# Eight buffers for gathered rows in the one-expert stage, gathers issued five items ahead with indices read straight from the table

## The reference, cut to what matters

```
xn    = layernorm(x)                       # x: 16384 tokens x 512
D     = fractal_dimension(xn); filt = wave_filter(D, 512)
x1    = ifft(fft(xn) * filt).real          # a circular filter along the 512 features
lat   = x1 @ W_el + b_el                   # 24 bits a token
s     = x1 + golay_correct(lat > 0) @ W_le + b_le
top   = top_k(softmax(xn @ router_w.T), 2) # two of 8 experts a token
f     = sum over the two of (xn @ W[e] + prob[e]) * weight[e]
out   = x + s * silu(f)
```

## Time and profile before

| | us |
|---|---|
| median of 3 executions (lowest, highest) | 1233.81 (1232.29, 1234.79) |
| the profiled execution | 1223.38 |
| its span in the trace | 1221.6 |
| PE busy, DVE busy, POOL busy, ACT busy | 1127.6, 1098.6, 873.8, 510.6 |
| mean granted TensorE clock | 0.972 |

### The profile page before, as it was taken

How to read it: one execution, slowest core, us unless ns; L and a number is a source line. 1 busy time by engine, 2 the same in 40 slices (tenths; PEclk the granted TensorE clock), 3 DMA queues, 4 the chain that set the end, 5 groups by cost and what they waited for, 6 DMA issues and landing times. The chain is left out here.

```text
span 1221.6 us, 26833 instructions
## 1 busy us (share of the span) xinstructions
PE 1127.6 (92%) x6283; PEld 607.5 (50%) x6284; DVE 1098.6 (90%) x2664; ACT 510.6 (42%) x1151; POOL 873.8 (72%) x857
## 2 busy tenths in 40 slices
PE   5998988627979999999999999999999999999996
PEld 4565555313434455555555555555555555555553
DVE  7899999999876889899999998999999899999985
ACT  4476775555754333333333333333333333333332
POOL 1136556748884778788888877888888788888874
PEclk9999999858999999999999999999999999999998
DMA  8669999213545776666666666676666666667663
GB/s 327 242 210 215 209 198 171 52 47 107 168 145 155 166 167 176 167 176 172 171 175 176 172 171 173 171 177 169 177 172 171 169 179 172 174 169 178 176 166 107
DMA packets 216921, 208.74 MB, mean 171 GB/s; under 512 B 166271, under 2 KB 166271, under 8 KB 212786
## 3 DMA queue, kind: packets, MB, share of 16 engines
q1 hardware_dynamic: 184370, 124.31, 42.5%
q0 software_dynamic: 31360, 79.78, 22.2%
q10 hardware_dynamic: 1152, 4.19, 1.2%
HBM read 123.36 MB, written 47.11 MB: 140 GB/s over the span
## 5 line engine op out<-in xcount | busy, mean ns | idle before, releaser
L1429 PE MATMUL banks<-w_hi,arena 128*128 (+1 forms) x1136 | 432.7, 381 | 5.8 <-DMA arena<-arena 4.4
L1430 PE MATMUL banks<-w_lo,arena 128*128 (+1 forms) x1136 | 432.1, 380 | 0.0
L1431 PE MATMUL banks<-w_hi,arena 128*128 (+1 forms) x1136 | 431.9, 380 | 0.0
L711 ACT ACTIVATE arena<-xbuf,inf 128x512 f16<-128x512 f32 x156 | 112.6, 722 | 529.8 <-DVE xbuf L1219 525.4
L526 POOL DMA_INDIRECT inf<-token_info,gidx x156 | 204.4, 1311 | 54.0 <-issue 53.4
L524 POOL DMA_INDIRECT xbuf<-in_L_attn_x,gidx x156 | 186.7, 1197 | 78.4 <-issue 65.6
L564 POOL TENSOR_TENSOR xbuf<-xbuf 128x512 f32<-128x512 f32 x128 | 162.7, 1271 | 36.0 <-DVE xbuf L1288 28.6
L503 POOL DMA_INDIRECT pair_tokens<-tok,slot x112 | 109.4, 977 | 104.9 <-DVE slot L1052 72.9
L1429 PEld LDWEIGHTS banks<-w_hi,arena 128*128 128x128 f16 x1136 | 111.4, 98 | 134.3 <-issue 15.9
L1431 PEld LDWEIGHTS banks<-w_hi,arena 128*128 128x128 f16 x1136 | 111.6, 98 | 131.1 <-issue 1.9
L530 POOL DMA_INDIRECT out<-xbuf,sidx x128 | 142.4, 1113 | 40.7 <-issue 40.4
(11 more groups left out here) (304 smaller groups left out, 1737.7 us busy)
## 6 DMA issues: line engine op xcount, KB each, us to landing
xbuf<-in_L_attn_x SPq DMA_DIRECT2D x32, 1024.0 KB, 11.6
arena<-extra_sums SPq DMA_DIRECT2D x128, 256.0 KB, 2.7
arena<-in_L_ffn_expert_weights SPq DMA_DIRECT2D x8, 1024.0 KB, 10.9
extra_sums<-arena SPq DMA_DIRECT2D x28, 256.0 KB, 3.0
token_info<-info ACTq DMA_DIRECT2D x8, 512.0 KB
xbuf<-in_L_attn_x,gidx POOLq DMA_INDIRECT x156, 3.9
inf<-token_info,gidx POOLq DMA_INDIRECT x156, 2.9
arena<-arena SPq DMA_TRANSPOSE x128
```

What stands on the lines that cost most here:

```text
L711: nc.scalar.activation(hi4[ring(i, k)], uv2[:, b], ACT.Copy, scale=inf2[:, k, 1:2]).then_inc(hi_ready, 1)
L1429: mm(ps, hi[:, c], wh, start=(c == 0), stop=False)
L1430: mm(ps, hi[:, c], wl, start=False, stop=False)
L1431: end = mm(ps, lo[:, c], wh, start=False, stop=(c == C - 1))
```

## The change

The one-expert stage gets four more buffers for gathered rows: item n sits in seat `n % 8`. The far four seats lie in memory that only the main stage and the routing use (`x2_far` where the main stage keeps `o2` and `ysb2`, `inf_far` in `lat`). POOL issues five gathers before the first coefficient, and `extra_prepare(n)` gathers item n+5. The wait for `split_ready` and for the coefficient is now for item n-3 (the occupant eight items earlier), and for a main item for the one four items earlier. The indices are read from `tile_tok` itself, so ACT's copies into `gidx` go in this stage, 32 of them, and stay in the main stage. Amounts of work on DVE, PE and SP are unchanged.

```diff
+        x2_far = xb[:, 2 * U * E:3 * U * E].rearrange("p (s e) -> p s e", s=U)
...
+        inf_far = lat[:, 0:2 * NE, :].rearrange("p n t -> p (n t)").rearrange("p (s w) -> p s w", s=U)
...
+        def seat(i, k):
+            return (i * U + k) % (2 * U) if extra(i) else k
...
-            def gather(k):
-                tokens = bass.IndirectOffsetOnAxis(ap=gidx[:, k:k + 1], axis=0)
...
+            def fetch(i, k, tokens):
+                tokens = bass.IndirectOffsetOnAxis(ap=tokens, axis=0)
+                pool.indirect_dma_start(out=x_at(i, k), out_offset=None, in_=x_rows, in_offset=tokens,
+                                        bounds_check=N - 1, oob_is_err=False).then_inc(ld_x2[seat(i, k)], 16)
+                pool.indirect_dma_start(out=inf_at(i, k), out_offset=None, in_=info_dram, in_offset=tokens,
+                                        bounds_check=N - 1, oob_is_err=False).then_inc(ld_x2[seat(i, k)], 16)
+            def gather(n):
+                earlier = n - 2 * U if n < NX else n - U
+                after(pool, split_ready, earlier + 1)
+                after(pool, coef_ready, earlier + 1)
+                fetch(n // U, n % U, tile_tok[:, n:n + 1])
...
             def extra_prepare(n):
                 if n + 1 < NX:
                     extra_coef(n + 1)
-                pool.wait_ge(gidx_ready, n + U + 1)
-                pool.wait_ge(split_ready, n + 1)
-                pool.wait_ge(coef_ready, n + 1)
-                gather(n % U)
+                if n + AHEAD < NX + U:
+                    gather(n + AHEAD)
...
-            for k in range(U):
-                pool.wait_ge(gidx_ready, k + 1)
-                gather(k)
+            AHEAD = U + 1
+            pool.wait_ge(tiles_ready, 1)
+            for n in range(AHEAD):
+                gather(n)
             pool.wait_ge(live_ready, 1)
             extra_coef(0)
...
-                if n + 3 < NX:
-                    gather_index(*at(n // U + 1, k, 3))
-                elif n + 3 < NX + 2:
+                if NX <= n + 3 < NX + 2:
                     bits_part(*at(n // U, k, 3))
```

More of the change, by code:

```diff
@@ L314, in build @@
             "rows_ready rows_loaded rows_float exps_mm toks_mm diag_ready spread_mm tiles_ready")
-        ld_x2 = [sem(f"ld_x2_{i}") for i in range(U)]
+        ld_x2 = [sem(f"ld_x2_{i}") for i in range(2 * U)]
         ld_e = [sem(f"ld_e{i}") for i in range(U)]
@@ L378, in parts_free, with x_at, inf_at, x_loads @@
                 eng.wait_ge(turned[k % 2], turns_before(i, k))
+        def seat(i, k):
+            return (i * U + k) % (2 * U) if extra(i) else k
+        def x_at(i, k):
+            r = seat(i, k)
+            return x2[:, r] if r < U else x2_far[:, r - U]
+        def inf_at(i, k):
+            r = seat(i, k)
+            return inf2[:, r] if r < U else inf_far[:, r - U]
+        def x_loads(i, k):
+            if extra(i):
+                return 32 * ((i * U + k) // (2 * U) + 1)
+            return 32 * (i - XR + (NX + U) // (2 * U) + 1)
         def at(i, k, ahead):
@@ L536, in extra_coef @@
                 k = n % U
-                pool.wait_ge(ld_x2[k], 32 * (n // U + 1))
+                pool.wait_ge(ld_x2[seat(n // U, k)], x_loads(n // U, k))
                 after(pool, x_scaled, n - U + 1)
                 c = 8 + PATH[n][1]
-                G.tensor_tensor(cab[:, k, 0:1], inf2[:, k, c:c + 1], tq[:, 7, n:n + 1], ALU.mult).then_inc(coef_ready, 1)
+                G.tensor_tensor(cab[:, k, 0:1], inf_at(n // U, k)[:, c:c + 1], tq[:, 7, n:n + 1], ALU.mult).then_inc(coef_ready, 1)
             def main_coef(i, k):
                 m = (i - XR) * U + k
-                pool.wait_ge(ld_x2[k], 32 * (i + 1))
+                pool.wait_ge(ld_x2[k], x_loads(i, k))
                 if not (first_main(i) and k < 2):
@@ L568, in step @@
                 if not last:
-                    pool.wait_ge(gidx_ready, j + U + 1)
+                    pool.wait_ge(gidx_ready, j - NX + 1)
                 pool.wait_ge(o_ready, m + 1)
@@ L572, in step @@
                 if not last:
-                    gather(k)
+                    fetch(XR, k, gidx[:, k:k + 1])
                 scatter_out(k)
-            for k in range(U):
-                pool.wait_ge(gidx_ready, k + 1)
-                gather(k)
+            AHEAD = U + 1
+            pool.wait_ge(tiles_ready, 1)
+            for n in range(AHEAD):
+                gather(n)
             pool.wait_ge(live_ready, 1)
@@ L699, in bits_part @@
                 b = k % 2
-                act.wait_ge(ld_x2[k], 32 * (i + 1))
+                act.wait_ge(ld_x2[k], x_loads(i, k))
                 parts_free(act, i, k)
@@ L710, in high_part @@
                 parts_free(act, i, k)
-                nc.scalar.activation(hi4[ring(i, k)], uv2[:, b], ACT.Copy, scale=inf2[:, k, 1:2]).then_inc(hi_ready, 1)
+                nc.scalar.activation(hi4[ring(i, k)], uv2[:, b], ACT.Copy, scale=inf_at(i, k)[:, 1:2]).then_inc(hi_ready, 1)
             def turned_copy(n):
@@ L752, in step @@
                     gather_index(i + 1, k)
-            act.wait_ge(tiles_ready, 1)
-            for k in range(U):
-                gather_index(0, k)
             act.wait_ge(pad_ready, 1)
@@ L1210, in halves_of @@
                 n, b = i * U + k, k % 2
-                dve.wait_ge(ld_x2[k], 32 * (i + 1))
+                x, inf = x_at(i, k), inf_at(i, k)
+                dve.wait_ge(ld_x2[seat(i, k)], x_loads(i, k))
                 after(dve, hi_ready, n - 1)
@@ L1224, in low_part @@
                 parts_free(dve, i, k)
[L1225 removed]
+                V.scalar_tensor_tensor(lo4[ring(i, k)], uv2[:, b], inf_at(i, k)[:, 1:2], hi4[ring(i, k)], ALU.mult,
                                        ALU.subtract).then_inc(split_ready, 1)
```

12 lines of the change are left out of this document (3 added, 9 removed).

## The result

The changed kernel took 1237.26 us (median of 20 runs) against 1231.98 us for before (20 runs beside them): ratio 1.0041, interval 1.0025 to 1.0057. The forecast was no change; it is slower by 0.4%.

What follows compares the result with a forecast made beforehand. POOL's instruction time was taken to pace the one-expert stage, the main stage only shifting. Seats 0, ACT 0, lead -0.3, coefficients 0 made 1223.1 us from 1223.38; plus 10.4 to the median, 1233.5 us, range 1227.0 to 1238.0.

Steps and rivals of the forecast that it cites:

- the frame of the sum: Whole kernel: the main stage only starts earlier or later, so only the end of the one-expert stage counts.
- More seats: POOL in the one-expert stage: removes waits for `split_ready` and an item's coefficient, but POOL never idles there; gain 0.
- Lead: POOL's one-expert gathers: earlier by some 0.7 us at most, from order and table indices, mostly absorbed behind DVE.
- the 0.3 us kept: One-expert stage: the gain taken for the earlier gathers, between 0 (all absorbed) and 0.7 us (none).
- Held instructions: POOL beside DVE in the one-expert stage: info gathers keep 2.73 us instead of 1.03; gathers of 5.79 and 4.24.
- New waits: Main items' gathers 28 to 31: still wait for a lower half of items 24 to 27; cost 0.
- the coefficients, 3.3 us in hand: POOL's coefficients in the one-expert stage: each one turn later, 3.3 us before ACT uses it; cost 0.
- B: One-expert stage: seats let gathers run ahead, removing PE waits and slow clock; 7.8 us, 1225.7; chance 0.32.
- partial case: One-expert stage: only one long POOL hold falls elsewhere or vanishes; 4.5 us, 1229; most of the 0.32 chance.
- C: One-expert stage: POOL is held longer or more often by DVE's run of work; 1236 to 1238; chance 0.21.

Runs made afterwards that it cites:

- e6: The kernel before, with the gathers of every second round of the one-expert stage raising four further semaphores; ratio 1.0041 (1.0021 to 1.006).
- e9: The changed kernel with the four load semaphores of before; eight seats, five ahead and table indices stay; ratio 1.0021 (1.0008 to 1.0034).
- e15: The changed kernel with before's four load semaphores and the first four main-stage gathers issued four items ahead; ratio 0.9999 (0.9987 to 1.0011).
- e2: The changed kernel run and traced again without an edit; ratio 1.0039 (1.0021 to 1.0056) against before.
- e18: e15 with DVE's two large table operations cut to the first of 128 tiles, output not the reference's; ratio 0.9961 (0.9935 to 0.9986).

## Why the prediction was wrong, point by point

**The step that failed** is the frame of the sum: "It can only start earlier or later, so the change is worth what it does to the end of the one-expert stage." The 4.655 us lie behind the main stage, in a row that the prediction never read. The sum had no term for it, none of the rivals was it, and the four added semaphores, which are part of the change, were put at nothing without a word. What the runs showed in its place is a DRAIN of POOL at the very end of 6.355 us for 1.700. e6 shows that four such semaphores suffice (1.0041), e9 and e15 that without them the drain is 1.70. Why the way in which gathers use semaphores lengthens a DRAIN some 800 us later stays open. Had one asked, the trace of before could not have given the price; that the closing DRAIN of POOL takes 1.7 us and all engines wait for it, it shows.

**More seats, gain 0: right.** POOL's waits after, 280 to 391 us:

```profile
POOL xbuf L544 <- POOL cab L567: 2.6, 3, 0.9
POOL xbuf L544 <- DVE arena L1246: 0.9, 1, 0.9
```

Up to gather 28 nothing but POOL's own length holds it, as in the earlier trace rows, and e15 puts the value of the whole stage change at nothing.

**Lead: mis-sized, and absorbed as forecast.** From the indices came what was forecast: the table is written at 270.44 + 0.32 and POOL starts 0.91 us later, where the earlier trace rows has 1.16, so 0.25 us for 0.2 to 0.3. But the whole lead was put at 0.7 us at most, and it was 2 to 3. Gather 4 is issued 13.61 us after the writing of the table, before 15.70. Here is gather 9, before, and gathers 9 and 14, after:

```profile
299.70 1.37 POOL L524 DMA_INDIRECT xbuf<-in_L_attn_x,gidx  x1
```

```profile
303.67 2.58 POOL L544 DMA_INDIRECT xbuf<-in_L_attn_x,tile_tok  x1
...
324.12 1.37 POOL L544 DMA_INDIRECT xbuf<-in_L_attn_x,tile_tok  x1
```

Counted from the writing of the table, gather 9 is at 35.86 us before and 32.91 after, gather 14 at 53.51 before (the first line of the earlier trace rows) and 53.36 after, 53.44 in e2. In e2 the lead is gone at gather 10 (40.75 for 40.71), where the prediction had it end, in the first profile by gather 14. So it is absorbed by the mechanism that the prediction gave, and the 0.3 us kept is not to be told from nothing.

**Held instructions: right in the first profile, not in the second.** The gather of the earlier trace rows with 5.79 us came again as 5.86, that with 4.24 as 4.25, and in place of the three info gathers of 2.73 us three of x take 2.58, among them gather 9 above:

```profile
348.11 5.86 POOL L546 DMA_INDIRECT lat<-token_info,tile_tok  x1 [0.31 <-issue]
...
360.47 4.25 POOL L544 DMA_INDIRECT xbuf<-in_L_attn_x,tile_tok  x1
```

In e2 the two are 3.32 and 3.20 us, and in place of the third of x an info gather takes 4.51.

In the first profile the waits, 310 to 391 us, answer to the earlier trace rows (14.6 and 10.5 us):

```profile
DVE xbuf L1236 <- DMA inf<-token_info,tile_tok: 11.4, 9, 3.7
PE banks L1461 <- DVE arena L1246: 11.1, 9, 3.0
DVE xbuf L1236 <- DMA lat<-token_info,tile_tok: 4.9, 4, 2.7
```

DVE's are 11.4 + 4.9 = 16.3 us. In e2 the like sums are 13.0 and 8.5. The slow clock of 0.94 in the third stretch did not come again (1.00 in both).

**New waits, cost 0: mis-sized.** They are three of 0.86 to 0.87 us for a coefficient and one of 0.86 for a lower half, not 0. The prediction looked at what is late behind them (the coefficients, 3.3 us in hand), and not at the gather that now stands directly behind a fresh coefficient, which the second order of its own section shows. Gather 31 is some 2 us later, and the stretch from the main stage's first matmul to its first addition is 2 us longer in all four profiles that have the waits; an earlier start of the main stage makes up for it, and no run shows for certain that any of it reaches the end.

**The rivals.** B's main case did not come: POOL had nothing to run ahead with. Its partial case, that the long holds depend on how POOL and DVE meet and may be shorter, is what e2 shows: 2.5 and 1.0 us less hold, and a main stage that begins 2.8 us earlier behind the first gather than in the first profile. But at the first addition it is no sooner than in before. C was wrong as the cause, since no further hold appears in the profile after, but e18 bears out its mechanism: there the hold is as long as DVE's unbroken run, not as one instruction. "SBUF — State Buffer" in the Trainium skill, Who interferes with whom, has the blocked engine wait for one instruction; the 5.74 us over twelve of at most 0.73 us are more than that, and the measurement decides.

**Level.** 1237.3 - 1233.5 = 3.8 us: the change cost 5.3 where -0.3 was forecast, and the kernel before came out 1.8 us lower than the 1233.8 that the forecast started from. That the time lies inside the range of 1227 to 1238, near the end that C gave, is luck: neither the range nor C contained this reason.

## What to carry to other kernels

Read a change also for what it leaves in the closing block: where, as here, a program's last wait is for GpSimd's transfers, its DRAIN stands on the path of every engine, and it was 1.7 to 6.8 us by which semaphores its gathers had raised hundreds of microseconds earlier. Let each transfer of a ring raise the same semaphore from the first stage to the last, and where a ring is made longer, first see whether the order already lets two seats share one. And when two profiles differ by more than the ratio, cut both at landmarks, take a second execution of each, and keep only what comes back and is not paid back in the piece beside it: here 13.8 us came down to 4.6.

## What the runs showed of the hardware

- POOL's closing DRAIN has exact, repeatable lengths, whether before takes 1226 or 1301 us beside it: 1700 ns for the nine semaphores of before, 2680 when four more are used steadily, 5865 to 6845 when the gathers of one place change their semaphore between rounds or stages; steps of 245 ns. Unused semaphores add nothing.
- A GpSimd gather that starts beside DVE's work was held over twelve DVE instructions, 5.74 us for 1.0 to 1.4, and ended within 1 us of DVE's first gap (e18).
- A gather directly behind a POOL instruction whose result it has to wait for starts 0.86 us after it, and 0.15 us after one that it need not wait for.
